# Reordering the opening of a fused AdaLN, spiking mixer and attention kernel on one core: first group, thresholds, a keep-warm run, and the norm of k

## The chip, the cores and the metric

The kernel runs on one core of one Trainium2 chip. A core has TensorE (PE in the profile, its weight loads PEld), VectorE (DVE), ScalarE (ACT), GpSimd (POOL) and SyncE (SP, which here only issues DMAs). The engines run their own instruction streams in program order and meet at semaphores. The metric is the device time of one execution in microseconds; lower is better.

## The reference, cut to what matters

```python
h = layernorm(x) * (1 + ca) + sa                      # x: 2 x 1024 tokens, 128 channels
r = sigmoid(h @ W_r.T + b_r); ek = exp(h @ W_k.T + b_k); v = h @ W_v.T + b_v
# scan over time, td = exp(b_td), g = exp(global_decay)
sa = ek*v + td*sa;  sb = ek + td*sb
inp = r * (g*ek*v + sa) / (g*ek + sb + 1e-6)
reset = mem - .05 > 0;  mem = .3*mem + inp - reset*.05;  spk = mem - .05 > 0
x = x + ga * spk
z = layernorm(x) * (1 + cb) + sb_
for layer in range(2):                                # local attention, 8 heads of 64, window 64
    q, k, v = split(shift_token(z) @ wqkv)
    q, k = l2norm(q) * qs, l2norm(k) * ks;  q, k = rotary_xpos(q, k)
    z = z + softmax(mask(8 * q @ k.T)) @ v @ wo
    z = z + gated_gelu_mlp(layernorm(shift_token(z)))
x = x + gb * z
# then a linear recurrent unit and a mixture of experts (8 experts, top 2), each with its own AdaLN
```

All arithmetic is float32. The change lies in the first block, up to the start of the attention, and in one wait of the attention.

## The kernel before

The 2048 tokens are cut into 4 groups of 512 columns (`g`) for the mixer and the MLPs, and into 16 tiles of 128 tokens (`n`) for the attention of each layer. Activations are stored with channels on the partitions. Every order of work is written out by hand, engine by engine; there is no scheduler.

**The mixer.** For each group, DVE computes the layer norm's statistics (`ln_stats`), POOL the reciprocal root (`ln_rstd`: a power on 128x4, L652, then a product, L653), ACT the normalization of four 128x128 blocks (`ln_norm`, L387), PE turns it back to channels (`ln_t2`), ACT applies the modulation (`mixer_out`, L393), PE makes the products with W_k and W_v (L1431, L1434), ACT the exponential and two scaled copies (L422, L425, L427), and DVE the two scans, the numerator and a reciprocal (from L943 to L957). The modulation vector itself comes from a small product (`modulation`, L1417) and eight small DVE instructions, which end in `mod_fin`. POOL also makes five scalars (`sc_ready`) ahead of its first `ln_rstd`. ACT runs groups 0 and 1 of `mixer_norm` and a table load ahead of `mixer_out(0)`.

**The membrane.** DVE runs four passes of 64 small instructions over 16 interleaved steps (L971, L975) and counts whether the last pass changed anything (L1012, L1013). A one-column product on PE (L1481) sums the count, DVE reads it into a register and branches to a fallback if it isn't zero. A threshold (`threshold`, 128x512) turns the steps into spikes times `ga`; DVE makes groups 0 and 1 (L1017) and POOL 2 and 3 (L777); DVE adds groups 0 and 1 to x (L1050), POOL 2 and 3 (`add_spikes`, L784). PE turns x for the next layer norm (`stack_t1`), the norm's way back is `ln_t2(ln_no(1, g))`, and `stack_out` (L393) writes z. `keep_clock` and `warm` are products without use that keep PE at work in gaps (L1470, L1410).

**The attention.** Per tile PE projects q, k and v (L1459, L1514), DVE multiplies by the rotary tables (L1079, L1082), POOL adds the two halves (`rope_sum`, L801, for k and q), ACT squares q and k, DVE sums the squares (L1093) and clamps them (`clamped`, L1100, then semaphore `ssq_max`), POOL raises them to -1/2 (`norms`, L809), DVE scales q (`q_normed`, L1108) and POOL scales k (`k_normed`, L817). PE turns q and k (`turn_qk`), makes the scores, DVE the maxima (`negmax`, L1114), ACT the exponentials (L515), PE turns them and multiplies with v (`weigh_v`, L1584). POOL's order for a tile is `norms`, a wait for `q_ready` (DVE's scaled q), `k_normed`, two `rope_sum` of the next tile. The first tiles run with a lead of three (`LEAD`): `n == 1 - LEAD` and `n == 2 - LEAD` are the two turns of the loop ahead of tile 0's `weigh_v`.

Of the kernel before, what the change touches and what calls it, by code (L numbers as in the profile page):

```python
# [12 lines left out]
ALU = mybir.AluOpType  # L13
# [8 lines left out]
NG = NTOK // GW  # L22
# [53 lines left out]
def program(nc, a, out):  # L76
    with ExitStack() as ctx:
# [6 lines left out]
        def sem(name):  # L84
# [97 lines left out]

        names = """ld_x0 ld_x1 ld_x2 ld_x3 ld_wm0 ld_wm1 ld_ew ld_c ld_wr ld_wa ld_wq ld_wl ld_lru ld_moe ld_out st_out
            init table edges mod_raw cnt_ready cnt_sum renewed spk hsA_dma1 hsA_dma2 hsA_dma3 silu_c mod_mm mod_fin sc_ready
# [187 lines left out]
        def _(act):  # L372
            act.dma_start(ident[:, :], a["ident"]).then_inc(s["ld_c"], 16)
            act.dma_start(vec[:, :], a["vec"]).then_inc(s["ld_c"], 16)
            own = Steps(act, s["act_own"])

            act.wait_ge(s["ld_c"], 32)
            act.activation(silc[:, :], vec[:, V_C:V_C + 4], ACT.Silu).then_inc(s["silu_c"], 1)
# [28 lines left out]
            def mixer_out(g):  # L407
# [3 lines left out]
                ln_out(ln_no(0, g), hsA[:, gsl(g)], mod[:, 0, CA, b:b + 1], mod[:, 0, SA, b:b + 1])  # L411

            mixer_norm(0)
            mixer_x(0)
            mixer_norm(1)
            act.wait_ge(s["init"], 2)
            load_table(ACT.Exp)
            mixer_out(0)
            for g in range(NG):

                act.wait_ge(s["kv_mm"], 2 * g + 1)
                own.one(act.activation(ek[:, gsl(g)], psS[:, g % 2, :], ACT.Exp, bias=vec[:, V_BK:V_BK + 1]))  # L422
                if g == 0:
                    act.wait_ge(s["sc_ready"], 1)
                act.activation(ek[:, gsl(g)], ek[:, gsl(g)], ACT.Identity, bias=0.0, scale=sc[:, 1:2]).then_inc(s["ek_ready"], 1)  # L425
                act.wait_ge(s["ek_ready"], g + 1)
                act.activation(gek[:, gsl(g)], ek[:, gsl(g)], ACT.Identity, bias=sc[:, 3:4], scale=sc[:, 2:3]).then_inc(s["gek_ready"], 1)  # L427
                if g + 1 < NG:
                    mixer_x(g + 1)
                    mixer_out(g + 1)  # L430
                if g + 2 < NG:
                    mixer_norm(g + 2)
# [204 lines left out]
        def _(pool):  # L637
# [33 lines left out]

            pool.wait_ge(s["ld_c"], 32)
            own.one(pool.memset(fr[:, 0:1], float(np.e)))
# [4 lines left out]
            pool.tensor_scalar(sc[:, 3:4], sc[:, 1:2], 1e-6, 0.0, ALU.mult, ALU.add).then_inc(s["sc_ready"], 1)  # L678
            ln_rstd(ln_no(0, 0))
            ln_rstd(ln_no(0, 1))  # L680
            for dst, src in ((4, V_NU), (5, V_TH), (6, V_GAM)):
# [90 lines left out]
            for k, edge in enumerate((hsA[64:128, T:T + 1], hsA[64:128, 0:1], hsM[64:128, T:T + 1], hsM[64:128, 0:1])):  # L772
                pool.memset(edge, 0.0).then_inc(s["edges"], 1)
                pool.wait_ge(s["edges"], k + 1)
            pool.wait_ge(s["cnt_ready"], 1)
            for g in (2, 3):
                pool.tensor_scalar(by_chunk(ekv, g), of_group(ph, g, 1), -1.0, mod[:, 0, GA, bof(g):bof(g) + 1],  # L777
                                   ALU.is_lt, ALU.mult).then_inc(s["spk"], 1)

            def add_spikes(g):  # L780

                pool.wait_ge(s["spk"], g - 1)
                pool.wait_ge(s["x_mixed"], g)
                pool.tensor_tensor(x_cm[:, gsl(g)], x_cm[:, gsl(g)], ekv[:, gsl(g)], ALU.add).then_inc(s["x_mixed"], 1)  # L784

# [34 lines left out]
            def attention(l, i):  # L820

                n = l * NT + i
                if has(i + 2):
                    norms(n + 2)
                    pool.wait_ge(s["q_ready"], n + 3)
                    k_normed(n + 2)
                if has(i + 3):
                    rope_sum(n + 3, 1)
                    rope_sum(n + 3, 0)
# [60 lines left out]
        def _(dve):  # L890
# [23 lines left out]
            mixer_stats(1)  # L914
            dve.wait_ge(s["ld_c"], 32)
            def modulation(k, bank):
# [105 lines left out]
            own.one(dve.tensor_copy(cnti[0:1, 0:1], psT1[0:1, 0:1]))  # L1022
            threshold(own, 1)
            changed = dve.value_load(cnti[0:1, 0:1], min_val=0, max_val=P * B * NCH)
            with dve.If(changed != 0):

                dve.wait_ge(s["cnt_ready"], 1)
                dve.wait_ge(s["spk"], 2)
                own.sync()
                again = [Steps(dve, s["fallback"]), Steps(dve, s["fallback_b"])]  # L1030
                for b in range(B):
                    again[b].did(dve.memset(vst[:, b, :], 0.0))
                changed = checked_pass(again)
                with dve.If(changed != 0):
                    with dve.Fori(0, NCH) as k:
                        for st in again:
                            st.enter(k, 2 * SEQ)
                        membrane_pass(again)
                    for st in again:
                        st.leave(NCH)  # L1040
                        st.sync()
                renewed = Steps(dve, s["renewed"])
                for g in range(NG):
                    threshold(renewed, g)
                renewed.sync()
# [8 lines left out]
            add_spikes(1)  # L1054
            for g in range(NG):
                ln(ln_no(1, g))

# [78 lines left out]
            dve.wait_ge(s["ln_out"], ln_no(1, 0) + 1)  # L1136
            shifted(hsA, z, 0, "hsA_ready")
            dve.wait_ge(s["rope_ready"], 4)
            qk_first(0)
# [234 lines left out]
        def _(pe):  # L1374
# [17 lines left out]

            pe.wait_ge(s["ld_c"], 32)

# [12 lines left out]
            def warm(times):  # L1407

                for _ in range(times):
                    mm(psO[:, 0, 0:P], ident[:, :], ident[:, :], start=True, stop=True)  # L1410

            mixer_turn(0)
            pe.wait_ge(s["silu_c"], 1)
# [6 lines left out]

            warm(6)
            modulation(0, psQK[:, 0, :])
            warm(4)

            ln_t2(ln_no(0, 0))
            pe.wait_ge(s["ld_wr"], 16)
            for g in range(NG):
# [61 lines left out]
            stack_t1(1)  # L1489
            keep_clock(2, psT1[:, :])  # L1490
            stack_t1(2)
            keep_clock(8, psT1[:, :])
            stack_t1(3)
            ln_t2(ln_no(1, 0))
            keep_clock(4, psT1[:, :])
# [19 lines left out]

            def turn_qk(l, i, between=None):

# [9 lines left out]
                four(psT0, lambda k: qkn[:, k * P:(k + 1) * P]).then_inc(s["qT_fill"], 1)  # L1527
                if between is not None:
                    between()
                pe.wait_ge(s["k_ready"], n + 1)  # L1530
# [75 lines left out]
            def attention(l, i):  # L1606
# [20 lines left out]
                if n == 1 - LEAD:  # L1627
                    proj_v(0, 0)
                    proj_part(0, 2, 1)
                    turn_qk(0, 0, lambda: proj_part(0, 2, 0))  # L1630
                    ln_t2(ln_no(1, NG - 1))
                elif early:
                    turn_qk(l, 0)
                    proj_v(l, 0)
                elif has(i + 2):
                    proj_v(l, i + 2)
                    turn_qk(l, i + 2)
                if i == NT - 1:
# [289 lines left out]
```

## Time and profile before

| | us |
|---|---|
| time before, median of 3 runs | 572.86 |
| lowest and highest of the three | 572.21, 574.23 |
| the profiled execution: its time | 573.93 |
| the profiled execution: its span | 572.1 |
| membrane passes, first instruction to the count | 49.8 to 85.8 |
| attention of layer 1, first to last `weigh_v` | 123.5 to 234.8 |
| attention of layer 2, first to last `weigh_v` | 295.4 to 408.2 |

Times in rows count from the start of the span. What lies around the span (573.93 less 572.1, 1.8 us) stays out of reach of the change. A row of the timeline is: start, length, engine, line, operation, output and inputs with their shapes, count of instructions merged into the row, and in brackets the idle time of the engine ahead of it and what ended it. For merged rows the length is that of the whole row.

### The profile page before, as it was taken

How to read it: one execution, taken by the hardware profiler on the slowest of the kernel's cores; microseconds unless marked ns; L12 is line 12 of the kernel's file. 1: busy time of each engine (PE TensorE's matmuls, PEld its weight loads, DVE VectorE, ACT ScalarE, POOL GpSimd, SP SyncE). 2: the span in 40 equal slices, each digit the busy share in tenths (PEclk: the TensorE clock that was granted, in tenths of full speed). 3: DMA queues.
4: the chain of work that ended last, by engine and by line, in shares of the span. 5: the costliest groups of instructions: out<-in, count | busy, mean ns of one | idle time of the engine just before them, and what ended most of it. 6: DMA issues, size and time to landing. Idle time of an engine off the chain costs nothing. (4 is left out here: it accounts for less than half of the span.)

```text
span 572.1 us, 11749 instructions
## 1 busy us (share of the span) xinstructions
PE 491.3 (86%) x4026; PEld 309.5 (54%) x4026; DVE 437.4 (76%) x1179; ACT 347.6 (61%) x1001; POOL 316.3 (55%) x257
## 2 busy tenths in 40 slices
PE   4741037889999999999989999999999998999995
PEld 4311013457777776543457777776544445667774
DVE  6699997879999995546899999995445687457775
ACT  4771002679999997543479999997646525533331
POOL 6551008788888888576888888884010275110000
PEclk9795558989999999999999999999999999999999
DMA  8400002221111112000031111111000000000000
GB/s 290 153 1 1 1 1 75 47 46 40 38 40 39 38 40 69 16 1 1 1 111 41 38 39 34 35 38 38 1 2 0 0 1 1 1 0 19 21 18 19
DMA packets 14832, 19.93 MB, mean 35 GB/s; under 512 B 2314, under 2 KB 8948, under 8 KB 14644
## 3 DMA queue, kind: packets, MB, share of 16 engines
q1 hardware_dynamic: 14484, 19.08, 12.2%
q8 instruction: 33, 0.54, 0.4%
q14 instruction: 27, 0.22, 0.1%
q10 hardware_dynamic: 288, 0.08, 0.1%
HBM read 8.94 MB, written 1.05 MB: 17 GB/s over the span
## 5 line engine op out<-in xcount | busy, mean ns | idle before, releaser
L515 ACT ACTIVATE prob<-psS,nmx 128x128 f32<-128x128 f32 x256 | 89.9, 377 | 19.8 <-DVE nmx L1114 19.8
L809 POOL TENSOR_TENSOR rn<-ssq,half 128x16 f32<-128x16 f32 x32 | 93.2, 2911 | 4.0 <-DVE ssq L1100 1.1
L801 POOL TENSOR_TENSOR ra<-ra,rb 128x512 f32<-128x512 f32 x64 | 80.1, 1273 | 2.7 <-DVE rb L1082 2.7
L652 POOL TENSOR_TENSOR rst<-mv,half 128x4 f32<-128x4 f32 x24 | 25.3, 1053 | 73.9 <-DVE mv L903 62.6
L1459 PE MATMUL psQK<-wqkv,hsA 128*128 128x512 f32 x128 | 62.2, 605 | 1.6 <-DVE hsA L1063 1.2
L515 ACT ACTIVATION_READ_ACCUMULATOR prob<-psS,nmx 128x1 f32 x256 | 55.4, 216 | 0.0
L1079 DVE TENSOR_TENSOR ra<-psQK,rope 128x512 f32<-128x512 f32 x64 | 43.9, 686 | 6.6 <-PE psQK L1459 5.9
L817 POOL TENSOR_TENSOR qkn<-ra,rn 128x512 f32<-128x512 f32 x32 | 33.3, 1042 | 26.4 <-DVE qkn L1108 26.4
L1114 DVE TENSOR_REDUCE nmx<-psS 128x4 f32<-128x512 f32 x64 | 41.1, 683 | 3.5 <-PE psS L1564 3.4
L1082 DVE TENSOR_TENSOR rb<-psQK,rope 128x512 f32<-128x512 f32 x64 | 43.6, 681 | 0.0
L633 ACT ACTIVATE gel<-psQK 128x512 f32<-128x512 f32 x32 | 19.1, 596 | 39.8 <-PE psQK L1772 39.8
L1378 PEld LDWEIGHTS psT<-ident,qkn 128*128 128x128 f32 x256 | 30.1, 142 | 24.1 <-issue 14.8
L1093 DVE TENSOR_REDUCE ssq<-sq 128x8 f32<-128x512 f32 x64 | 41.1, 676 | 1.1 <-ACT sq L455 0.9
L387 ACT ACTIVATE lnx<-psS,nmr,rst 128x128 f32<-128x128 f32 x20 | 7.5, 456 | 55.2 <-POOL nmr L653 55.2
L489 ACT ACTIVATE pT<-psT 128x512 f32<-128x512 f32 x64 | 36.4, 654 | 4.9 <-PE psT L1378 4.9
L1378 PE MATMUL psT<-ident,qkn 128*128 128x128 f32 x256 | 34.6, 276 | 5.0 <-DVE qkn L1108 3.8
L1584 PE MATMUL psO<-vAB,pT 128*64 128x64 f32 x1024 | 36.9, 225 | 1.6 <-ACT pT L489 1.6
L1378 PEld LDWEIGHTS psT<-ident,prob 128*128 128x128 f32 x256 | 29.8, 140 | 15.0 <-issue 14.4
L1470 PE MATMUL psO<-masks,identb 128*128 128x512 bf16 x22 | 7.8, 527 | 33.5 <-DVE vAB L975 33.5
L1584 PEld LDWEIGHTS psO<-vAB,pT 128*64 128x64 f32 x1024 | 32.4, 138 | 7.7 <-ACT pT L489 5.6
L1514 PE MATMUL psO<-wqkv,hsA 128*128 128x512 f32 x64 | 35.8, 641 | 0.0
L1108 DVE TENSOR_TENSOR qkn<-ra,rn 128x512 f32<-128x512 f32 x32 | 22.1, 691 | 16.9 <-POOL rn L809 16.8
(238 smaller groups left out, 1203.7 us busy)
## 6 DMA issues: line engine op xcount, KB each, us to landing
vAB<-vAB SPq DMA_DIRECT2D x62, 128.0 KB, 2.2
wqkv<-in_wqkv SPq DMA_DIRECT2D x2, 768.0 KB, 8.2
big<-in_x SPq DMA_DIRECT2D x4, 256.0 KB, 4.6
ropeb<-in_rope SPq DMA_DIRECT2D x1, 1024.0 KB, 6.4
big<-in_ew SPq DMA_DIRECT2D x2, 512.0 KB, 4.2
out<-big SPq DMA_DIRECT2D x4, 256.0 KB, 2.3
wmod<-in_wmod SPq DMA_DIRECT2D x2, 384.0 KB, 5.9
w<-in_w SPq DMA_DIRECT2D x2, 341.0 KB
```

The source lines that it names most:

```text
L489: act.activation(pT[:, 4 * hb:4 * hb + 4, :], four((psT0, psT1)[hb]), ACT.Copy).then_inc(s["pT_evac"], 1)
L515: act.activation(prob[:, k, :], psS[:, hb, c * P:(c + 1) * P], ACT.Exp, bias=nmx[:, k:k + 1], accum_out=sums[:, n % 2, k:k + 1]).then_inc( ...
L801: pool.tensor_tensor(o, o, rb[:, r], ALU.add).then_inc(s["sum_" + name], 1)
L809: pool.tensor_tensor(rn[:, :], ssq[:, :], half[:, :], ALU.pow).then_inc(s["rn_ready"], 1)
L1079: dve.tensor_tensor(heads(o), heads(psQK[:, part, :]), rope[:, at8, 2 * part, :].unsqueeze(1).to_broadcast([P, H, DH]), ALU.mult).then_inc ...
L1082: dve.tensor_tensor(rb[:, r].rearrange("p (h a d) -> p h a d", h=H, a=2), psQK[:, part, :].rearrange("p (h a d) -> p h a d", h=H, a=2)[:, ...
L1093: dve.tensor_reduce(ssq[:, 8 * part:8 * part + 8], heads(sq[:, part * INNER:(part + 1) * INNER]), AX.X, ALU.add).then_inc(s["ssq_" + name], 1)
L1114: dve.tensor_reduce(nmx[:, 4 * hb:4 * hb + 4], psS[:, hb, :].rearrange("p (h k) -> p h k", h=4), AX.X, ALU.max, negate=True).then_inc(s["n ...
L1378: i = pe.transpose(dst[:, k * P:(k + 1) * P], src(k), ident[:, :])
L1459: mm(psQK[:, part, :], hsA[:, tile(i)], wqkv[:, part * INNER:(part + 1) * INNER], start=True, stop=True).then_inc(s[name + "_mm"], 1)
L1514: mm(psO[:, 1, :], hsA[:, tile(i)], wqkv[:, 2 * INNER:3 * INNER], start=True, stop=True).then_inc(s["v_fill"], 1)
L1584: j = mm(psO[64 * w:64 * w + 64, 0, h * DH:(h + 1) * DH], pT[:, slot(h), 64 * w:64 * w + 64], (vA, vB)[w][:, u, h * DH:(h + 1) * DH], star ...
```

## The change

It has these parts:

- **First group.** ident has a semaphore of its own (`ld_id`), so PE waits for it alone; three `warm` products go ahead of the first turn, three ahead of the modulation, two behind `ln_t2(0)` in place of four ahead of it. POOL runs `ln_rstd` 0 and 1 ahead of its scalars. ACT loads the table first and runs `mixer_norm(1)` behind group 0's exponential and copies instead of ahead of `mixer_out(0)`.
- **Thresholds.** All four on DVE: 0, 1 and 2 around the reading of the count, 3 behind the statistics of group 0; POOL keeps the adds of groups 2 and 3. The statistics of group 3 go behind the shift of group 0.
- **First way back.** `ln_t2(ln_no(1, 0))` goes ahead of `stack_t1(3)`; `keep_clock` runs of 2 and 8 are joined to one of 10 ahead of it.
- **Into the attention.** `keep_clock(3)` ahead of the first `turn_qk`, q's projection of tile 2 behind it; `ln_t2(ln_no(1, 3))` moves one turn later, behind the first scores; `keep_clock(8)` ahead of the second `turn_qk`.
- **Norm of k.** POOL's wait for `q_ready` ahead of `k_normed` is gone, in both layers.

```diff
@@ scalar
-            mixer_norm(0)
-            mixer_x(0)
-            mixer_norm(1)
-            act.wait_ge(s["init"], 2)
-            load_table(ACT.Exp)
+            act.wait_ge(s["init"], 1)
+            load_table(ACT.Exp)
+            mixer_norm(0)
+            mixer_x(0)
             mixer_out(0)
...
+                if g == 0:
+                    mixer_norm(1)
                 if g + 1 < NG:
@@ gpsimd
-            pool.wait_ge(s["ld_c"], 32)
+            ln_rstd(ln_no(0, 0))
+            ln_rstd(ln_no(0, 1))
+            pool.wait_ge(s["ld_c"], 16)
...
-            ln_rstd(ln_no(0, 0))
-            ln_rstd(ln_no(0, 1))
...
-            pool.wait_ge(s["cnt_ready"], 1)
-            for g in (2, 3):
-                pool.tensor_scalar(by_chunk(ekv, g), of_group(ph, g, 1), -1.0, mod[:, 0, GA, bof(g):bof(g) + 1],
-                                   ALU.is_lt, ALU.mult).then_inc(s["spk"], 1)
-
             def add_spikes(g):
 
-                pool.wait_ge(s["spk"], g - 1)
                 pool.wait_ge(s["x_mixed"], g)
+                if g == 3:
+                    pool.wait_ge(s["spk"], 1)
...
                     norms(n + 2)
-                    pool.wait_ge(s["q_ready"], n + 3)
                     k_normed(n + 2)
@@ vector
             threshold(own, 1)
+            threshold(own, 2)
             changed = dve.value_load(cnti[0:1, 0:1], min_val=0, max_val=P * B * NCH)
...
-            for g in range(NG):
-                ln(ln_no(1, g))
+            ln(ln_no(1, 0))
+            threshold(Steps(dve, s["spk"]), 3)
+            ln(ln_no(1, 1))
+            ln(ln_no(1, 2))
...
             shifted(hsA, z, 0, "hsA_ready")
+            ln(ln_no(1, 3))
@@ tensor
-            pe.wait_ge(s["ld_c"], 32)
+            pe.wait_ge(s["ld_id"], 16)
...
+            warm(3)
             mixer_turn(0)
...
-            warm(6)
+            warm(3)
             modulation(0, psQK[:, 0, :])
-            warm(4)
-
             ln_t2(ln_no(0, 0))
+            warm(2)
...
-            keep_clock(2, psT1[:, :])
             stack_t1(2)
-            keep_clock(8, psT1[:, :])
+            keep_clock(10, psT1[:, :])
+            ln_t2(ln_no(1, 0))
             stack_t1(3)
-            ln_t2(ln_no(1, 0))
             keep_clock(4, psT1[:, :])
...
                 if n == 1 - LEAD:
                     proj_v(0, 0)
                     proj_part(0, 2, 1)
-                    turn_qk(0, 0, lambda: proj_part(0, 2, 0))
-                    ln_t2(ln_no(1, NG - 1))
+                    keep_clock(3, psT1[:, :])
+                    turn_qk(0, 0)
+                    proj_part(0, 2, 0)
...
                 elif has(i + 2):
+                    if n == 2 - LEAD:
+                        ln_t2(ln_no(1, NG - 1))
                     proj_v(l, i + 2)
+                    if n == 2 - LEAD:
+                        pe.wait_ge(s["kT_evac"], 1)
+                        keep_clock(8, psT1[:, :])
                     turn_qk(l, i + 2)
```

## Rows read from the trace of the kernel before

**Rows 1.** Waits of POOL, whole span: us in total, times, longest

```profile
POOL qkn L817 <- DVE qkn L1108: 26.4, 32, 1.3
```

**Rows 2.** Timeline, one tile of layer 1 in the attention

```profile
164.05 2.91 POOL L809 TENSOR_TENSOR rn<-ssq,half 128x16 f32<-128x16 f32 x1
...
166.99 0.69 DVE L1108 TENSOR_TENSOR qkn<-ra,rn 128x512 f32<-128x512 f32 x1 [0.28 <-POOL rn L809]
...
167.06 1.15 PE L1584 MATMUL psO<-vAB,pT 128*64 128x64 f32 x32
...
167.76 1.04 POOL L817 TENSOR_TENSOR qkn<-ra,rn 128x512 f32<-128x512 f32 x1 [0.81 <-DVE qkn L1108]
...
168.76 2.50 POOL L801 TENSOR_TENSOR ra<-ra,rb 128x512 f32<-128x512 f32 x2
...
171.01 0.29 DVE L1100 TENSOR_SCALAR ssq<-ssq 128x16 f32<-128x16 f32 x1
...
171.38 2.91 POOL L809 TENSOR_TENSOR rn<-ssq,half 128x16 f32<-128x16 f32 x1
...
174.32 1.15 PE L1584 MATMUL psO<-vAB,pT 128*64 128x64 f32 x32
```

**Rows 3.** Timeline, two tiles of layer 2, PE's products with v

```profile
303.64 1.15 PE L1584 MATMUL psO<-vAB,pT 128*64 128x64 f32 x32
...
310.96 1.15 PE L1584 MATMUL psO<-vAB,pT 128*64 128x64 f32 x32
```

**Rows 4.** Timeline, the mixer's first group and the start of its second

```profile
5.71 0.16 DVE L903 TENSOR_SCALAR mv<-mv 128x4 f32<-128x4 f32 x1
...
7.55 1.04 POOL L652 TENSOR_TENSOR rst<-mv,half 128x4 f32<-128x4 f32 x1
...
8.90 1.65 ACT L387 ACTIVATE lnx<-big,nmr,rst 128x128 f32<-128x128 f32 x4 [3.76 <-POOL nmr L653]
...
13.99 0.76 ACT L393 ACTIVATE hsA<-psT,mod 128x512 f32<-128x512 f32 x1
...
14.89 1.94 PE L1431 MATMUL psS<-hsA,wrkv 128*128 128x512 f32 x2 [3.63 <-ACT hsA L393]
...
17.59 0.72 ACT L425 ACTIVATE big<-big,sc 128x512 f32<-128x512 f32 x1
...
18.58 0.76 DVE L943 SCALAR_TENSOR_TENSOR psO<-psO,vec,big 128x512 f32<-128x512 f32 x1 [4.72 <-PE psO L1434]
...
20.36 1.12 PE L1431 MATMUL psS<-hsA,wrkv 128*128 128x512 f32 x2 [0.94 <-ACT hsA L393]
...
25.67 0.67 DVE L943 SCALAR_TENSOR_TENSOR psO<-psO,vec,big 128x512 f32<-128x512 f32 x1
```

**Rows 5.** Timeline, from the thresholds to the first z

```profile
85.99 5.80 POOL L777 TENSOR_SCALAR big<-vAB,mod 128x512 f32<-128x512 f32 x2 [40.02 <-DVE cnt L1013]
...
86.51 1.47 DVE L1017 TENSOR_SCALAR big<-vAB,mod 128x512 f32<-128x512 f32 x1
...
91.04 0.89 DVE L897 BATCH_NORM_STATS2 st<-psS 128x6 f32<-128x128 f32 x4
...
92.97 1.03 POOL L652 TENSOR_TENSOR rst<-mv,half 128x4 f32<-128x4 f32 x1
...
93.59 3.54 PE L1470 MATMUL psT<-masks,identb 128*128 128x512 bf16 x8
...
98.05 0.78 ACT L393 ACTIVATE z<-psO,mod 128x512 f32<-128x512 f32 x1 [2.23 <-PE psO L1378]
```

**Rows 6.** Timeline, first norm of the attention and first product with v

```profile
105.55 2.91 POOL L809 TENSOR_TENSOR rn<-ssq,half 128x16 f32<-128x16 f32 x1 [0.36 <-DVE ssq L1100]
...
123.55 1.15 PE L1584 MATMUL psO<-vAB,pT 128*64 128x64 f32 x32
```

**Rows 7.** Timeline, late in the kernel: two instructions that read SBUF twice, together

```profile
466.21 0.69 DVE L1272 TENSOR_TENSOR big<-z,big 128x512 f32<-128x512 f32 x1
466.25 1.78 POOL L867 TENSOR_TENSOR big<-z,tsin 128x512 f32<-128x512 f32 x1 [2.02 <-DVE z L1267]
```

More of the change, by code:

```diff
@@ L181, in program @@
         psT1 = ps("psT1", [P, GW])
-        names = """ld_x0 ld_x1 ld_x2 ld_x3 ld_wm0 ld_wm1 ld_ew ld_c ld_wr ld_wa ld_wq ld_wl ld_lru ld_moe ld_out st_out
+        names = """ld_id ld_x0 ld_x1 ld_x2 ld_x3 ld_wm0 ld_wm1 ld_ew ld_c ld_wr ld_wa ld_wq ld_wl ld_lru ld_moe ld_out st_out
             init table edges mod_raw cnt_ready cnt_sum renewed spk hsA_dma1 hsA_dma2 hsA_dma3 silu_c mod_mm mod_fin sc_ready
@@ L372, in _ @@
         def _(act):
-            act.dma_start(ident[:, :], a["ident"]).then_inc(s["ld_c"], 16)
+            act.dma_start(ident[:, :], a["ident"]).then_inc(s["ld_id"], 16)
             act.dma_start(vec[:, :], a["vec"]).then_inc(s["ld_c"], 16)
             own = Steps(act, s["act_own"])
-            act.wait_ge(s["ld_c"], 32)
+            act.wait_ge(s["ld_c"], 16)
             act.activation(silc[:, :], vec[:, V_C:V_C + 4], ACT.Silu).then_inc(s["silu_c"], 1)
@@ L914, in _ @@
             mixer_stats(1)
-            dve.wait_ge(s["ld_c"], 32)
+            dve.wait_ge(s["ld_c"], 16)
             def modulation(k, bank):
@@ L1027, in _ @@
                 dve.wait_ge(s["cnt_ready"], 1)
-                dve.wait_ge(s["spk"], 2)
                 own.sync()
@@ L1042, in _ @@
                 renewed = Steps(dve, s["renewed"])
-                for g in range(NG):
+                for g in range(NG - 1):
                     threshold(renewed, g)
@@ L1054, in _ @@
             add_spikes(1)
-            for g in range(NG):
-                ln(ln_no(1, g))
+            ln(ln_no(1, 0))
+            threshold(Steps(dve, s["spk"]), 3)
+            ln(ln_no(1, 1))
+            ln(ln_no(1, 2))
             def shifted(dst, src, g, name):
@@ L1514, in proj_v, with turn_qk @@
                 mm(psO[:, 1, :], hsA[:, tile(i)], wqkv[:, 2 * INNER:3 * INNER], start=True, stop=True).then_inc(s["v_fill"], 1)
-            def turn_qk(l, i, between=None):
+            def turn_qk(l, i):
                 n = l * NT + i
@@ L1527, in turn_qk @@
                 four(psT0, lambda k: qkn[:, k * P:(k + 1) * P]).then_inc(s["qT_fill"], 1)
-                if between is not None:
-                    between()
                 pe.wait_ge(s["k_ready"], n + 1)
```

## The prediction, made before the result was seen

> **What bounds the kernel now.** I read the timeline stage by stage, since the change touches an opening that runs in chains (0 to 124 us) and one wait of the attention. The chain that ended last reaches back only to the expert stage, which stays as it is, so an early gain moves the end only if nothing between absorbs it. In the membrane passes DVE alone works; they shift as a block.
>
> In the attention three loops nearly coincide. PE's own tile is 174.32 - 167.06 = 7.26 us, with no wait shown [rows 2]. POOL's tile is 171.38 - 164.05 = 7.33: the power 2.91, then 0.81 of waiting until DVE has scaled q, k's norm 1.04, two sums 2.50, and the clamp, which got in only when the second sum had ended at 171.26 [rows 2]. That wait comes to 26.4 us over 32 tiles [rows 1], but PE could give at most 7.33 - 7.26 a tile back. In layer 2 PE's tile is 7.32, paced by that loop [rows 3].
>
> **The first group.** GpSimd starts the power of group 0 at 7.55, though the statistics were there at 5.87; its scalars stood ahead [rows 4]. With the order turned it starts at 5.95, the normalization at 7.3 instead of 8.90, and ends at 8.95 [rows 4]. The table load now lies ahead of that, in ACT's idle time (3.76 us there). The way back on PE is over at about 9.7; `mod_fin` is there at about 10.1 by my estimate: PE starts when ident has landed and not vec, and the modulation, with one turn and six `warm` products ahead of it as now, moves up by that, some 0.8. So `mixer_out(0)` starts at 10.1 instead of 13.99: 3.9 less. Here nothing of group 1 and no table load stands between. PE's first pair of products took 1.94 for k after 3.63 us of idleness, and 1.12 in the second group [rows 4]; with `warm` and no such gap the engine stays at the upper clock level, some 0.9 less (bounds 0 and 1.6). From 10.1: 0.76, product 1.1, exponential and copy 1.4 give 13.4 for DVE's first instruction, against 18.58. What is late next is the second group: DVE needs 25.67 - 18.58 = 7.09 for a group and would be ready at 20.5, but ACT has then run group 1's normalization (1.65), its modulation, group 2's normalization (1.65) and the exponential, and I add it up to 20.95. From there on DVE is the bound as before, and I take **4.7 us** (25.67 - 20.95; bounds 3.5 and 5.2). The scalars, now behind the powers, end at about 11.5, with ACT asking at 12.7. The copy of x needs neither.
>
> **Thresholds and the first way back.** Two thresholds held GpSimd to 91.79 [rows 5]; then came its first add, and the power of the attention's first norm at 92.97, while its statistics were over at 91.04, where the next group's begin [rows 5]. On DVE the third threshold costs 0.7, but the second took 1.47 while GpSimd worked on the same tile, and should take 0.7 alone, so DVE's adds start where they did. If reading the register and branching was hidden under those 1.47 and shows again behind the third, up to 0.7 is lost. DVE's two adds, behind 86.51 + 1.47 = 87.98 at some 0.65 each, end at 89.3 [rows 5]; GpSimd then adds group 2 until 90.7 (1.25, the length of its sums [rows 2]) and is free: the power starts at 91.1, 1.85 earlier, and the normalization is over at 93.95. The eight useless products took 3.54 [rows 5], at the lower clock level after a gap; without it ten take 2.3 and end at 93.5, in front of `ln_t2(ln_no(1, 0))`, which no longer waits for `stack_t1(3)`. z starts at 94.7 instead of 98.05 [rows 5], 3.35 less. DVE has threshold 3 (0.7 to 1.5) and two statistics to finish by 95.5 and just does; group 3's statistics (1.6) then fill the gap in which it waited for PE, at a cost of 0.1. I take **3.3 us** up to the first power on `rn`, 102.25 instead of 105.55 [rows 6]; bounds 1.6 (branch and a late threshold) and 4.0.
>
> **The wait ahead of k's norm.** It goes in 32 places, but not its whole 0.81 us comes back. Both instructions read SBUF twice (the sums or ra, and rn). [Rows 7] show such a pair: DVE started 0.04 us ahead and took its usual 0.69, GpSimd took 1.78 and ended 1.13 behind DVE's end; a GpSimd instruction of that shape takes 1.25 [rows 2]. So it was blocked, and only its 0.1 to 0.2 of start-up ran under the other.
> That is what the Trainium skill, SBUF — State Buffer, Who interferes with whom, states: a DVE instruction with two SBUF inputs and a GpSimd instruction that reads SBUF exclude each other, and whichever starts first holds the shared ports throughout. By this rule each tile gets 0.1 to 0.2 back; by rows 2 read without it, 0.8. The trace agrees with the rule.
> DVE starts 0.03 us behind the power's end (164.05 + 2.91 = 166.96, then 166.99) [rows 2]; GpSimd starts 0.08 behind what releases it (the clamp ends at 171.01 + 0.29 = 171.30, the power starts at 171.38) [rows 2]. So DVE goes first where it is waiting, and k's norm ends 0.2 earlier. POOL's loop becomes about 7.2 (7.33 less 0.15), DVE's through the clamp is the same, and PE paces all at 7.26. That is worth 0.07 for the last five tiles of layer 1 and 14 of layer 2: 0.35 and 1.0.
>
> In the lead-in of layer 1 each of two powers comes 0.1 to 0.2 earlier, `keep_clock(8)` saves a stretch at the lower level on PE, but DVE's clamp, maxima and ACT's exponentials, which now stand behind z of group 3, gain only 3.2. The first loops pass through these, so of the possible 5 us at 123.55 [rows 6] I keep 3.65 a tile later: **0.35** more (bounds -1.0 and +2.5, the latter if the 0.8 came back each time). In layer 2's lead-in DVE is behind with the MLP when the power ends; there GpSimd goes first, and q is blocked for up to 1.04 [rows 2]: **-0.6** (bounds -1.6 and +0.6).
>
> **Sum.** 4.7 + 3.3 + 0.35 + 0.35 + 1.0 - 0.6 = 9.1 us. The profiled execution, 573.93 (span 572.1 and 1.8 around it), would be 564.8. It lies 1.1 above the median of the runs, 572.86, so the prediction is 572.86 - 9.1 = 563.8.
>
> **Rivals.**
> *The port turned against q.* Should GpSimd win at the power's end, where 0.05 us decides, q's scaling starts 1.1 later in each tile, and DVE's loop, 7.2 with that scaling in it, becomes 8.3. Over 30 tiles that is 30 x 1.0 = 30 us against today's 7.33: 572.9 - 9 + 30, about 592. For it speaks that both wait for the same instruction; against it the 0.03 against 0.08, and that DVE works on tables and then waits 0.28 [rows 2]. It decides from the point at which DVE's start falls behind by 0.05 in more than ten tiles. Chance 0.07. The same rule in the Trainium skill (SBUF — State Buffer, Who interferes with whom) gives this too, since there the order decides.
> *No exclusion.* The pair runs together and k's norm ends 0.8 earlier: lead-ins give 2.5 and 0.6 instead of 0.35 and -0.6, so 572.9 - 12.5 = 560.4. Against it are rows 7. Chance 0.10.
> *The second gain is absorbed.* The branch shows behind the third threshold (0.7), threshold 3 stands in front of the statistics with GpSimd's powers beside it (1 us), and the lead-in falls to the lower clock (1 to 1.5): 3 to 3.5 less, 567.2. For it: DVE is on the path throughout that stretch. Chance 0.20.
> *The change doesn't do what it says.* Group 1's later normalization makes DVE wait for group 1 as long as it gained on group 0 and the thresholds only change engine: 572 to 573. ACT's sum for group 1 is within 0.5 us of DVE's, so it would take a further 4 us that no row shows. Chance 0.03.
>
> **How the numbers follow.** My forecast has 0.60, with 561.8 to 566 as its own range. To this the range adds the absorbed case and the case without exclusion, nearly whole: 560.5 to 568, holding about 0.85 (0.60 + 0.20 + part of 0.10). The port turned against q and no effect stay outside. A measurement of this kernel tells about 0.3% (1.7 us) from no change. Faster: 0.60 + 0.10 + 0.20 + what of the rest is a mild form = 0.91; same 0.03; slower 0.06.
>
> **What would show it.** In the profile after: `mixer_out(0)` at about 10.1, DVE's group 1 at about 21, the first membrane instruction near 45.1 instead of 49.8; the power of the first attention norm 1.8 earlier against the count and z 3.3; no useless product above 0.3 us before z; k's norm with a length near 1.7 where it starts within 0.1 us of q's, and ending 0.2 earlier against the power; PE's tile 7.26 in both layers. The prediction is wrong if q's norm is seen starting behind k's (tile above 7.4), if DVE's adds start more than 0.5 later against the count, or if DVE waits for ACT in group 1.

## The result, and the profile after

| | before | after |
|---|---|---|
| time, median of 4 runs | 572.57 | 566.70 |
| lowest and highest | 572.21, 574.23 | 566.26, 567.15 |
| the profiled execution: time and span | 573.93, 572.1 | 566.38, 564.4 |
| start of the membrane's count (its last instruction) | 85.5 | 82.9 |
| first power on `rn` | 105.55 | 99.94 |
| layer 1, first to last `weigh_v` | 123.5 to 234.8 | 115.9 to 227.8 |
| layer 2, first to last `weigh_v` | 295.4 to 408.2 | 288.8 to 400.4 |

The ratio of after to before is 0.9895, with an interval of 0.988 to 0.991: faster by 1.0%, 5.9 us between the medians (the median of before is now over one run more than at the time of the forecast). The forecast was 563.8 with a range of 560.5 to 568.0. The time lies in the range, but 0.7 above the likeliest case's own range (561.8 to 566), near the 567.2 of the absorbed case. The prediction also named a wait of DVE for ACT in group 1 as a sign of being wrong; the profile shows one of 0.18 us, at 22.93 below.

In the timeline after, the first group (answers to [rows 4]); the clock record of this trace begins at 15.56 with the upper level:

```profile
6.05 1.02 POOL L653 TENSOR_TENSOR rst<-mv,half 128x4 f32<-128x4 f32 x1 [4.30 <-DVE mv L899]
...
7.39 1.65 ACT L387 ACTIVATE lnx<-big,nmr,rst 128x128 f32<-128x128 f32 x4 [0.90 <-POOL nmr L654]
...
10.67 0.15 DVE L923 COPY zero<-mod 128x1 f32<-128x1 f32 x1
...
10.86 0.78 ACT L393 ACTIVATE hsA<-psT,mod 128x512 f32<-128x512 f32 x1 [1.34 <-DVE zero L923]
...
11.78 2.04 PE L1430 MATMUL psS<-hsA,wrkv 128*128 128x512 f32 x2 [0.35 <-ACT hsA L393]
...
13.62 1.91 PE L1433 MATMUL psO<-hsA,wrkv 128*128 128x512 f32 x2
...
15.57 0.76 DVE L939 SCALAR_TENSOR_TENSOR psO<-psO,vec,big 128x512 f32<-128x512 f32 x1 [1.82 <-PE psO L1433]
...
22.93 0.76 DVE L939 SCALAR_TENSOR_TENSOR psO<-psO,vec,big 128x512 f32<-128x512 f32 x1 [0.18 <-ACT big L424]
```

The normalization starts 1.5 earlier, about as forecast. Two things eat into it: `mixer_out(0)` waits 1.34 for the modulation vector, and both products take nearly twice what the product with W_k takes at the upper level of TensorE's clock (2.04 and 1.91 against 1.12 in [rows 4]). DVE waits for the second of them.

The timeline after, from the thresholds to the first power on `rn` (answers to [rows 5, 6]):

```profile
83.87 1.30 DVE L1013 TENSOR_SCALAR big<-vAB,mod 128x512 f32<-128x512 f32 x2
...
85.47 1.29 DVE L1046 TENSOR_TENSOR x_cm<-x_cm,big 128x512 f32<-128x512 f32 x2 [0.30 <-DVE big L1013]
...
86.91 1.26 POOL L781 TENSOR_TENSOR x_cm<-x_cm,big 128x512 f32<-128x512 f32 x1 [43.14 <-DVE x_cm L1046]
...
88.40 0.69 DVE L1013 TENSOR_SCALAR big<-vAB,mod 128x512 f32<-128x512 f32 x1
88.57 1.41 POOL L653 TENSOR_TENSOR rst<-mv,half 128x4 f32<-128x4 f32 x1 [0.40 <-DVE mv L899]
...
88.72 2.32 PE L1469 MATMUL psT<-masks,identb 128*128 128x512 bf16 x10
...
90.21 1.26 POOL L781 TENSOR_TENSOR x_cm<-x_cm,big 128x512 f32<-128x512 f32 x1
...
90.34 1.16 DVE L898 TENSOR_SCALAR nmean<-mv 128x4 f32<-128x4 f32 x1
...
92.55 0.78 ACT L393 ACTIVATE z<-psO,mod 128x512 f32<-128x512 f32 x1 [0.75 <-PE psO L1377]
...
99.94 2.91 POOL L806 TENSOR_TENSOR rn<-ssq,half 128x16 f32<-128x16 f32 x1 [0.28 <-DVE ssq L1098]
```

Against the count, z is 98.05 - 92.55 - 2.6 = 2.9 earlier. The second and third threshold take 1.30 together, reading the register and branching show 0.30 behind them, and the ten useless products take 2.32 at the upper level (the granted clock is 1.00 from 83.8 to 99.9).

The timeline after, one tile of layer 1 (answers to [rows 2]):

```profile
128.42 2.91 POOL L806 TENSOR_TENSOR rn<-ssq,half 128x16 f32<-128x16 f32 x1 [0.21 <-DVE ssq L1098]
...
131.36 0.69 DVE L1106 TENSOR_TENSOR qkn<-ra,rn 128x512 f32<-128x512 f32 x1 [0.31 <-POOL rn L806]
...
131.40 1.15 PE L1580 MATMUL psO<-vAB,pT 128*64 128x64 f32 x32
131.40 1.55 POOL L814 TENSOR_TENSOR qkn<-ra,rn 128x512 f32<-128x512 f32 x1
...
132.91 2.50 POOL L798 TENSOR_TENSOR ra<-ra,rb 128x512 f32<-128x512 f32 x2
...
135.38 0.17 DVE L1098 TENSOR_SCALAR ssq<-ssq 128x16 f32<-128x16 f32 x1
...
135.63 2.90 POOL L806 TENSOR_TENSOR rn<-ssq,half 128x16 f32<-128x16 f32 x1 [0.21 <-DVE ssq L1098]
...
138.66 1.15 PE L1580 MATMUL psO<-vAB,pT 128*64 128x64 f32 x32
```

The wait of 26.4 us [rows 1] is gone, and k's norm now takes 1.55 and not 1.04: it starts 0.04 behind q's and mostly stands still until that is over. From the power's start to its end it is 4.53 against 4.75 in [rows 2], 0.22 earlier. POOL's tile is 7.21 and PE's 7.26.

q's norm keeps its 0.68 to 0.69 in 31 of the 32 tiles. In the second tile of layer 2 GpSimd was first by 0.02, and q's norm was the one that was blocked:

```profile
282.12 1.04 POOL L814 TENSOR_TENSOR qkn<-ra,rn 128x512 f32<-128x512 f32 x1
282.14 1.57 DVE L1106 TENSOR_TENSOR qkn<-ra,rn 128x512 f32<-128x512 f32 x1
```

### The profile page after: what moved, and what is told of

Same layout as the page of the kernel before. It is cut to its first block and busy times, and to the rows that moved or that the text cites. A ratio compares the mean times of both kernels' runs of the same rounds, so it can differ in the third digit from the quotient of the medians.

```text
span 564.4 us, 11730 instructions
## 1 busy us (share of the span) xinstructions
PE 491.8 (87%) x4033; PEld 310.3 (55%) x4033; DVE 436.7 (77%) x1181; ACT 348.3 (62%) x1001; POOL 328.7 (58%) x255
## 5 line engine op out<-in xcount | busy, mean ns | idle before, releaser
L814 POOL TENSOR_TENSOR qkn<-ra,rn 128x512 f32<-128x512 f32 x32 | 49.5, 1548 | 2.5
L1377 PEld LDWEIGHTS psT<-ident,prob 128*128 128x128 f32 x256 | 29.8, 140 | 14.8 <-issue 14.3
L1215 DVE SCALAR_TENSOR_TENSOR hg<-psO,vec,gel 128x512 f32<-128x512 f32 (+1 forms) x24 | 17.2, 745 | 20.9 <-ACT gel L569 20.9
```

Source lines behind the costliest of these rows:

```text
L814: pool.tensor_tensor(heads(qkn[:, INNER:]), heads(ra_k[n % 2]), rn[:, 8:16].unsqueeze(2).to_broadcast([P, H, DH]), ALU.mult).then_inc(s["k ...
L1377: i = pe.transpose(dst[:, k * P:(k + 1) * P], src(k), ident[:, :])
```

## The experiments

Each was compared with the kernel before on its own chip; the ratios are to that. Marks in the traces (count, first power on `rn`, first and last `weigh_v`) are read as in the table above.

**The parts alone, on the kernel before.** First the wait ahead of k's norm:

```diff
                     norms(n + 2)
-                    pool.wait_ge(s["q_ready"], n + 3)
                     k_normed(n + 2)
```

> The kernel before with only the wait for q_ready ahead of k's norm taken out, both layers. Theory 1 (the two norms exclude each other at SBUF, q's goes first): k's norm grows from 1.04 to about 1.55 us and ends only 0.3 earlier against the power; PE's tile in layer 2 goes from 7.33 to 7.26, 1.0 to 1.2 us over the layer, and the time falls by 1 to 2 us. Theory 2 (they run side by side): k's norm keeps 1.04, the power's period in the lead-ins falls to 6.5, the time falls by 3.5 us or more.

Measured: 572.99 against 573.01, ratio 0.9996 (0.9985 to 1.0008). k's norm is 1.55 long here too. Layer 2 takes 111.6 instead of 112.8, as expected, but the stretch between the layers is 0.7 longer and layer 1 is unchanged; no gain can be told, where 1 to 2 us were expected. GpSimd was first in three of the 32 tiles, two of them in the first four of layer 1, and q's norm took 1.39 to 1.57 there. In the profiled execution the mixer's first DVE instruction stood at 17.7, not at 18.58.

The first group's edits alone (the diff's lines on `ld_id`, the order of POOL's scalars, table and `mixer_norm(1)` on ACT, `warm`):

> The kernel before with only the mixer's first group reordered (ident's own semaphore, warm 3+3+2, powers ahead of the scalars, table first, group 1's normalization behind group 0's copies). Theory 1: DVE's first mixer instruction comes 3 us earlier (15.6 instead of 18.6), its chain runs without waits from there and everything behind is shifted: 2.7 us less. Theory 2 (given back later): the count comes 2.7 earlier, but PE's clock level falls in other places of the lead-in and at most 1 us is left at the end.

Measured: 570.96, ratio 0.9958 (0.9945 to 0.9972), 2.4 us, near the 2.7 of theory 1. DVE started at 15.5 and the count came at 82.9, both as in the changed kernel.

The thresholds, `keep_clock(10)`, `ln_t2(ln_no(1, 0))` ahead of `stack_t1(3)` and the later statistics of group 3 alone:

> The kernel before with only the thresholds on DVE, group 3's statistics behind the shift, ten keep_clock products and the first way back ahead of the fourth turn. Theory 1: from the count to the first power on rn 3.0 us less (20.0 before), as in the changed kernel, and 2.5 to 3 us at the end. Theory 2 (absorbed in the lead-in, where other things bound): 3.0 to the first power, under 1.5 at the end.

Measured: 571.24, ratio 0.9961 (0.9949 to 0.9973), 2.2 us, a little under theory 1. The first power on `rn` came 17.1 behind the count, as in the changed kernel, instead of 20.0.

The way into the attention alone (`keep_clock(3)` and `(8)`, `ln_t2(ln_no(1, 3))` a turn later):

> The kernel before with only the edits on PE in the lead-in of layer 1 (keep_clock 3 and 8, q's projection of tile 2 behind the first turn, group 3's way back one turn later). Theory 1: the second keep-warm run saves the stretch at the lower clock ahead of the first product with v, 1 us, and z of group 3, now behind the first scores on ACT, gives most of it back: 0 to 1 us less. Theory 2: z of group 3 on ACT costs more than the clock gives: up to 1 us more.

Measured: 573.33, ratio 0.9999 (0.9989 to 1.001). The first `weigh_v` came 1.6 earlier against the count (36.4 instead of 38.0) and layer 1 took 1.6 more (112.9 instead of 111.3): the head start was handed back at POOL's 7.33 a tile.

The four ratios leave 0.42 + 0.39 + 0.04 + 0.01 = 0.86%, 4.9 us, against 6.0 by the ratio together. The missing 1.1 us is within the intervals, but the next run shows an interaction of two parts of about that size.

**The changed kernel with the wait put back.**

```diff
                     norms(n + 2)
+                    pool.wait_ge(s["q_ready"], n + 3)
                     k_normed(n + 2)
```

> The changed kernel with the wait for q_ready ahead of k's norm put back. Theory 1 (the lead-in's 1.5 us stays only if the loop of GpSimd is a little faster than PE's): layer 1 from first to last product with v grows from 111.9 to about 113, layer 2 from 111.6 to 112.8, the seam between the layers gets 0.5 shorter; 568.3 to 568.8. Theory 2 (the wait has nothing to do with it, as alone it gave nothing measurable): 566.5 to 567.

Measured: 568.41, ratio 0.9927 (0.9911 to 0.9944). Taking the wait away is worth 0.32%, 1.8 us, here. Layer 1 takes 112.8 with it and 111.9 without, layer 2 112.8 and 111.6. Alone, taking the wait away was worth 0.04% and changed nothing in layer 1. Behind the edits of the way into the attention, with which GpSimd's loop of 7.33 sets the pace from the first tiles on, it gives 0.9 there. That is the interaction of the two parts; by the ratios it is 0.28%, 1.6 us, with an uncertainty nearly as large.

**q's norm made to start second.** The changed kernel, and the same edit in the kernel of the run above as a control:

```diff
                 dve.wait_ge(s["rn_ready"], n + 1)
+                own.one(dve.memset(zero[:, 0:1], 0.0))
                 dve.wait_ge(s["sum_q"], n + 1)
```

> The changed kernel with one small VectorE instruction (a memset of one column, and the wait for it) between the power's end and q's norm, so that k's norm on GpSimd starts first. Theory 1 (exclusive ports, the first to start holds them): q's norm starts or ends about 1.0 later against the power, VectorE's loop has 8.2 to 8.3 us a tile, PE's tile follows, 25 to 30 us more: 592 to 597. Theory 2 (order does not matter, or the two share the ports in parts): only the small instruction is paid, 0.15 us a tile at most, 567 to 569.

> Control for q_second: the same small VectorE instruction with the wait for q_ready put back, so that q's norm is later by it but never against k's. Both theories: 0.15 us a tile on the loop of GpSimd, 7.33 to about 7.5: 571 to 573.

Measured: 589.89, ratio 1.0306 (1.0283 to 1.0329), and for the control 572.26, ratio 0.9995 (0.9983 to 1.0007). The timeline of the first, one tile:

```profile
154.53 2.90 POOL L806 TENSOR_TENSOR rn<-ssq,half 128x16 f32<-128x16 f32 x1 [1.23 <-DVE ssq L1098]
...
157.50 0.06 DVE L1103 MEMSET zero<- 128x1 f32 x1 [0.42 <-POOL rn L806]
157.51 1.04 POOL L814 TENSOR_TENSOR qkn<-ra,rn 128x512 f32<-128x512 f32 x1
157.59 1.51 DVE L1107 TENSOR_TENSOR qkn<-ra,rn 128x512 f32<-128x512 f32 x1
...
162.68 2.91 POOL L806 TENSOR_TENSOR rn<-ssq,half 128x16 f32<-128x16 f32 x1 [1.22 <-DVE ssq L1098]
```

Now GpSimd has its usual 1.04 and DVE takes 1.51 for its 0.69. The tile is 8.15 instead of 7.25, and the time lies 2 us below the range of theory 1 (592 to 597). The instruction in front costs 3.9 us where the order is held (572.26 less 568.41); where it turns the order it costs 23.2 (589.89 less 566.70). The order of two starts, 0.08 apart, is worth 19 us here. By this the exclusion of [rows 7] is shown for this pair too, and so is the price of the rival of the port turned against q (592 forecast), which only a few hundredths of a microsecond keep away. The Trainium skill's rule (SBUF — State Buffer, Who interferes with whom) is borne out in both orders.

**Why the first group started at 15.6 and not at 13.4.** The changed kernel with the modulation straight behind the first turn:

```diff
-            warm(3)
             modulation(0, psQK[:, 0, :])
+            warm(6)
             ln_t2(ln_no(0, 0))
             warm(2)
```

> The changed kernel with the modulation's products straight behind the first turn and six warm products behind them, ahead of ln_t2(0), instead of three ahead of the modulation. Theory 1 (the first group is bound by mod_fin and then by PE at the lower clock level): mod_fin comes 0.7 to 1.3 earlier, and six products in a row right ahead of the group's own raise the level before the product with W_k; VectorE's first mixer instruction at 13.5 to 14.5 instead of 15.6, 1 to 2 us less in the end (564.7 to 565.7). Theory 2 (the second group's chain on ScalarE is next): VectorE then waits for the exponential of group 1, and 0.5 at most is left.

Measured: 567.75, ratio 0.9914 (0.9896 to 0.9932): no gain. Its timeline:

```profile
8.17 2.91 PE L1409 MATMUL psO<-ident 128*128 128x128 f32 x12
...
9.36 0.15 DVE L923 COPY zero<-mod 128x1 f32<-128x1 f32 x1
...
10.87 1.06 PE L1377 MATMUL psT<-ident,lnx 128*128 128x128 f32 x4
...
12.04 0.78 ACT L393 ACTIVATE hsA<-psT,mod 128x512 f32<-128x512 f32 x1 [2.55 <-PE psT L1377]
...
12.96 1.10 PE L1430 MATMUL psS<-hsA,wrkv 128*128 128x512 f32 x2 [0.34 <-ACT hsA L393]
...
15.65 0.76 DVE L939 SCALAR_TENSOR_TENSOR psO<-psO,vec,big 128x512 f32<-128x512 f32 x1 [3.21 <-ACT big L424]
```

In this execution the vector is there at 9.51 and the product with W_k is at the upper level, 1.10 long, as theory 1 has it. But the six useless products stood in front of the way back until 10.87. So they were split, which brings the run to the point:

```diff
-            warm(3)
             modulation(0, psQK[:, 0, :])
+            warm(2)
             ln_t2(ln_no(0, 0))
-            warm(2)
+            warm(3)
```

> The changed kernel, with the modulation straight behind the first turn, two useless products behind it (four passes, some 1.0 us, until about 9.1, when the normalization of group 0 is over) and three behind the way back; one useless product less in all than now. With six of them behind the modulation nothing was gained, and I hold that those six, twelve passes of 2.91 us, stood themselves in front of the way back. My theory: mod_fin at about 9.5, way back over at about 10.2, mixer_out(0) at 10.3 instead of 10.86, PE at work without a gap from 5.75 to 11.2, so that the product with W_k takes 1.10 as with six of them (and not 2.04); DVE's first mixer instruction 3.6 behind mixer_out(0), at about 13.9 instead of 15.57, and 565.2 to 565.7 us, 1.2 less than the changed kernel (0.2 to 0.4 of the 1.7 is lost where DVE waits for ACT in the second group). Rival one: the start stays at 15.6, since fewer passes keep the granted clock at the lower level until 15.5: 566.4 to 566.9. Rival two: DVE starts at 13.9 and waits for ACT in group 1 as long as it gained: 566.4 as well, with a wait of over 1 us ahead of group 1.

Measured: 566.23, ratio 0.9893 (0.9876 to 0.9911). Its timeline:

```profile
10.29 0.78 ACT L393 ACTIVATE hsA<-psT,mod 128x512 f32<-128x512 f32 x1 [0.86 <-PE psT L1377]
...
11.26 1.57 PE L1430 MATMUL psS<-hsA,wrkv 128*128 128x512 f32 x2
...
14.43 0.76 DVE L939 SCALAR_TENSOR_TENSOR psO<-psO,vec,big 128x512 f32<-128x512 f32 x1 [1.97 <-ACT big L424]
...
18.80 3.35 DVE L953 RECIPROCAL big<-big 128x512 f32<-128x512 f32 x1 [0.44 <-POOL big L704]
...
22.07 0.67 DVE L939 SCALAR_TENSOR_TENSOR psO<-psO,vec,big 128x512 f32<-128x512 f32 x1
...
22.78 1.99 DVE L945 TENSOR_TENSOR_SCAN big<-sc,big 128x512 f32<-128x512 f32 x1
```

DVE starts 1.14 earlier than in the changed kernel, but the count comes only 0.2 earlier (82.7), and the time is the same. The expected loss to ACT is not there; a third engine, GpSimd, takes the gain. The reciprocal of group 0 waits 0.44 for GpSimd's denominator (L704), and the scan of group 1, which started at 23.72 and took 1.28 in the changed kernel, falls beside GpSimd's rotary tables and takes 1.99. That the split itself brought DVE's earlier start is not shown. Seven profiled executions, each of a different kernel, have the changed kernel's own opening. In four DVE started at 15.4 to 15.6 (the changed kernel, the first group alone, the wait put back, the kernel without the way into the attention), in three at 14.5 (both kernels with the memset, and the next one). The opening of the next kernel:

```profile
9.04 0.66 PE L1377 MATMUL psT<-ident,lnx 128*128 128x128 f32 x4 [0.38 <-ACT lnx L387]
...
9.90 0.78 ACT L393 ACTIVATE hsA<-psT,mod 128x512 f32<-128x512 f32 x1 [0.43 <-DVE zero L923]
...
10.83 1.96 PE L1430 MATMUL psS<-hsA,wrkv 128*128 128x512 f32 x2 [0.68 <-ACT hsA L393]
...
14.52 0.76 DVE L939 SCALAR_TENSOR_TENSOR psO<-psO,vec,big 128x512 f32<-128x512 f32 x1 [1.72 <-PE psO L1433]
```

The way back takes 0.66 here against 1.09 in the changed kernel's trace, and the modulation vector is there at 9.87 and not at 10.82: in this execution TensorE was already at the upper level. Then PE stood idle for 0.68, and the granted clock is 0.50 from 10.9 to 14.3. Its reciprocal of group 0 waited 0.59 for GpSimd and its scan of group 1 took 1.97, so it lost the earlier start in the same two places. The count came at 82.6 in the three early executions and at 82.9 to 83.6 in the four others.

**Threshold 3 one group later.**

```diff
             ln(ln_no(1, 0))
-            threshold(Steps(dve, s["spk"]), 3)
             ln(ln_no(1, 1))
+            threshold(Steps(dve, s["spk"]), 3)
```

> The changed kernel, with threshold 3 behind the statistics of group 1 instead of group 0. My theory: in the changed kernel it ran beside the power of group 0's norm (1.41 long and not 1.03) and pushed GpSimd's add of group 3 onto the negated mean of group 1, which took 1.16. With it one group later the power takes 1.03, the normalization of group 0 and z come 0.4 earlier (z 2.5 less than before by the count, now 2.87 after 5.5 against 2.63), and the end 0.4: 566.2 us against 566.7, which five rounds can hardly tell; the lengths of the power and of the negated mean decide. Rival one: the threshold, now beside GpSimd's power again or beside the add, only moves the block to another instruction: z the same, 566.7. Rival two: group 3's add comes later and with it the fourth way back: 567.2.

Measured: 566.44, ratio 0.9895 (0.9877 to 0.9913). Its timeline:

```profile
88.31 1.02 POOL L653 TENSOR_TENSOR rst<-mv,half 128x4 f32<-128x4 f32 x1 [0.40 <-DVE mv L899]
...
89.48 0.17 DVE L898 TENSOR_SCALAR nmean<-mv 128x4 f32<-128x4 f32 x1
...
89.63 0.69 DVE L1013 TENSOR_SCALAR big<-vAB,mod 128x512 f32<-128x512 f32 x1
...
91.90 0.78 ACT L393 ACTIVATE z<-psO,mod 128x512 f32<-128x512 f32 x1 [0.75 <-PE psO L1377]
```

The power is back to 1.02 and the negated mean to 0.17. From DVE's two adds (85.22 here) to z it is 6.68 instead of 92.55 - 85.47 = 7.08, the 0.4 of the theory. The time agrees with the theory but can't be told from no change.

**The changed kernel without the edits of the way into the attention.**

```diff
-                    keep_clock(3, psT1[:, :])
-                    turn_qk(0, 0)
-                    proj_part(0, 2, 0)
+                    turn_qk(0, 0, lambda: proj_part(0, 2, 0))
+                    ln_t2(ln_no(1, NG - 1))
...
-                    if n == 2 - LEAD:
-                        ln_t2(ln_no(1, NG - 1))
                     proj_v(l, i + 2)
-                    if n == 2 - LEAD:
-                        pe.wait_ge(s["kT_evac"], 1)
-                        keep_clock(8, psT1[:, :])
```

> The changed kernel without the edits of the way into the attention (the old order of the two turns ahead of tile 0's product with v, no keep_clock(3) and keep_clock(8)); first group, thresholds and k's norm are as changed. Alone on the kernel before, those edits gained 1.5 us up to the first product with v and gave it back in layer 1 (112.8 instead of 111.3), where I hold GpSimd's loop with k's wait to set 7.3 a tile. My theory: with the wait gone layer 1 takes the gain on: without the edits the first product with v comes 1.5 later against the count and layer 1 takes 111.3 instead of 111.9, so 0.9 us more than the changed kernel, 567.6. Rival: the edits are worth nothing here as well, 566.7 (first product with v 1.5 later, layer 1 at 110.4).

Measured: 567.49, ratio 0.9908 (0.989 to 0.9926). The time is the one expected, the way to it is not. The first `weigh_v` came 33.5 behind the count and not 34.5 (33.0 in the changed kernel), layer 1 took 111.4, and the stretch between the layers was 62.5 instead of 61.0, with the granted clock at the lower level from 284.7 to 288.1, which the changed kernel's trace does not have there. GpSimd was first in three tiles of this execution (110.64, 282.85 and 290.34), with q's norm 1.38 to 1.57 long, and in one of the changed kernel's, so part of the longer stretch between the layers is q's norm blocked. What these edits are worth beside the others stays open: 0.8 us by the medians, with intervals that overlap.

**GpSimd relieved in the mixer.** The two better variants together, and GpSimd's work that is not wanted yet moved out of the way:

```diff
@@ gpsimd, in place of ahead of the powers of groups 2 and 3
                 if g == 0:
-                    rope_tables(0)
+                    rope_tables(0, range(3))
                 if g == 1:
                     quotient(0)
+                    rope_tables(0, range(3, 4))
+                    for dst, src in ((4, V_NU), (5, V_TH), (6, V_GAM)):
+                        own.did(pool.tensor_tensor(sc[:, dst:dst + 1], fr[:, 0:1], vec[:, src:src + 1], ALU.pow))
+                    own.sync()
+                    own.one(pool.tensor_scalar(fr[:, 2:3], sc[:, 4:5], -1.0, 0.0, ALU.mult, ALU.add))
+                    own.one(pool.tensor_tensor(sc[:, 7:8], fr[:, 0:1], fr[:, 2:3], ALU.pow))
```

> The changed kernel with the split useless products (modulation, two, way back, three) and threshold 3 behind the statistics of group 1, and besides with GpSimd relieved in the mixer: the five scalars of the recurrent unit (2.4 us) go out of the way of the denominator of group 0 to behind the quotient of group 0, and of the four rotary tables the last goes there too, so that none lies beside the scan of group 1. With the split alone DVE began 1.14 earlier and the count came only 0.2 earlier: the reciprocal of group 0 waited 0.44 for GpSimd's denominator and the first scan of group 1 took 1.99 and not 1.24. My theory: GpSimd was what came late next, so now the reciprocal of group 0 has no wait and starts at 18.3, the scan of group 1 takes 1.24, DVE's groups start at 14.4, 21.6, 28.7 and 35.8 and the count is at 81.3 to 81.6 instead of 82.9; with 0.35 more from the threshold the first power on rn comes at 98.1 instead of 99.9 and the time is 564.9, 1.8 less than the changed kernel. Rival: ACT and PE come late next, DVE waits for the exponential of group 1 or 2 by as much, the count is at 82.6 and the time 566.1.

Measured: 565.54, ratio 0.9869 (0.9853 to 0.9886), from four runs: 565.33, 565.47, 565.61 and, the profiled one, 567.13. It is the lowest of all the kernels here, 7.5 us under before by the ratio; its interval still touches that of the changed kernel. The trace is of the slowest of the four and shows both theories at work:

```profile
18.94 3.34 DVE L954 RECIPROCAL big<-big 128x512 f32<-128x512 f32 x1
...
23.24 0.76 DVE L940 SCALAR_TENSOR_TENSOR psO<-psO,vec,big 128x512 f32<-128x512 f32 x1 [0.95 <-PE psO L1434]
...
24.03 1.28 DVE L946 TENSOR_TENSOR_SCAN big<-sc,big 128x512 f32<-128x512 f32 x1
...
36.27 0.63 ACT L437 ACTIVATE big<-big 128x512 f32<-128x512 f32 x1
...
37.04 3.48 POOL L694 TENSOR_TENSOR z<-big 128x512 f32<-128x512 f32 x2 [2.00 <-ACT big L437]
...
42.99 3.35 DVE L954 RECIPROCAL big<-big 128x512 f32<-128x512 f32 x1 [1.59 <-POOL big L699]
```

The reciprocal of group 0 has no wait and the scan of group 1 takes 1.28: GpSimd was what came late. But DVE started at 15.11 in this execution, where the same order of work on PE gave 14.43 in the run with the split products, and the granted clock is 0.50 from 16.9 to 23.7; PE's products for group 1 took 2.08 and 1.92 in it, and DVE waited 0.95 for them; the sigmoids followed late, GpSimd's two products behind them took 3.48 and held up the denominator of group 3 for 1.59. The count came at 84.0 in this execution. Whether the other three, 1.5 to 1.8 faster, had the count at 81.5 no trace shows.

## Why the prediction was right, and what it got wrong

By the profiled executions the gain is 573.93 - 566.38 = 7.55 us, by the medians 5.9; 9.1 was forecast. That the time still fell inside the range is in part luck: the first group was forecast 2 us too high, and the attention about 1 us too low.

- **The first group: mis-sized, 4.7 forecast, 2.7 measured** (25.67 - 22.93; 2.6 at the count). GpSimd, the table load and group 1's normalization went as forecast. Of the 2.17 by which DVE's start missed 13.4, the vector accounts for 0.76 (`mixer_out(0)` at 10.86, not 10.1): the modulation's products took 2.56, where they took 1.40 in the kernel before. The product with W_k took 2.04 where I had put 1.1. My sentence "with `warm` and no such gap the engine stays at the upper clock level" failed: PE was at work nearly without a gap from 3.49 to 11.43, and it still ran the pair at 2.04. Another 0.3 is the product with W_v, at the lower level as well, on which DVE waited and not on the exponential. In the three executions with the same opening that started DVE at 14.5, the vector came in time (`mixer_out(0)` at 9.90 to 9.95), but the product with W_k took 1.89 to 1.96 all the same. So about half of the 2.17 belongs to the execution, and the rest to a clock level that the forecast had too high. The first membrane instruction came at 47.2 instead of 49.8; 45.1 was forecast.
- **"From there on DVE is the bound as before" fails for any earlier start**, and that weighs more than the late start. With a start at 14.4 the count moved by 0.2. GpSimd's denominator and its tables beside the scan take the rest. I take from this that even a start at 13.4 would not have given 20.95 for group 1; no run shows such a start. I had added up ACT's work for group 1, and not GpSimd's for group 0.
- **Thresholds and first way back: right, 3.3 forecast, 3.0 measured** (105.55 - 99.94 - 2.64). The adds start where they did, the branch shows with 0.30 (up to 0.7 allowed for), the ten products took 2.32 (2.3 forecast), z came 2.9 earlier against the count (3.35). The 0.4 missing is threshold 3 beside the power: with it moved, z came 3.3 earlier.
- **Layer 1: too low, and by another way.** I kept 0.35 for the lead-in and 0.35 for the end: 0.7 from the first power on `rn` to the last `weigh_v`. It was 7.0 - 5.6 = 1.4: the first `weigh_v` came 7.7 earlier, and layer 1 gave back 0.6. PE paces it at 7.26 as forecast.
- **Layer 2: +1.0 and -0.6 forecast, +0.8 measured** (408.2 - 400.4 less 7.0). Within the layer it is 1.2, between the layers -0.4, and nothing after it is lost.
- **k's norm: right.** Blocked, 1.55 long, ending 0.22 earlier, q first by 0.04, POOL's tile 7.21. The case without exclusion is out, since k's norm would have kept its 1.04. The port turned against q in one tile of 32, in the lead-in of layer 2, where the forecast had it; in the other 31 it did not, and the memset turned it in every tile. The forecast of 592 for that case is mis-added: 572.9 - 9 + 30 is 593.9.
- **The profile's execution as the base: wrong by about 1.** I took 9.1 from the median, as if the 1.1 by which that execution lay above the median were spread evenly. Much of it lay in the opening which the change replaces: DVE's first mixer instruction stood at 18.58 there, and at 17.7, 17.5 and 18.0 in the profiles of the three kernels above that keep this opening (the wait, the thresholds and the way into the attention alone). From 17.7 there is 0.9 less to gain.

So the shortfall of 3.2 us against the medians is 2.1 (first group) + 0.3 (thresholds) - 1.0 (more gained in the attention) + 1.8, the rest, which is nearly all the base: the profiled execution of before lay 1.4 above its median over four runs, that of after 0.3 below. The rival of the second gain absorbed came nearest in time, but it was the first gain that was absorbed: the second came nearly whole.

## What to carry to other kernels

When an early stage is sped up on one engine, add up all the engines that feed the next instruction of the bound, the one with spare time too; and look at what their work will then lie beside, since two instructions that exclude each other only cost where they meet. Removing a wait between two such instructions gives back a start-up time and not the wait, and leaves the order to a race of a few hundredths of a microsecond which here costs ten times the gain (19 us against 1.8). And do not subtract a sum made in one execution from a median before asking in which stage that execution was slow.

## What the runs showed of the hardware that was not expected

- Two instructions that both read SBUF twice: GpSimd second gives 1.55 for its 1.04, DVE second 1.51 for its 0.69; each starts 0.04 to 0.08 behind the other and ends 0.90 and 0.55 behind it, so only 0.14 of its own length runs beside the first.
- A DVE instruction on 4 columns took 1.16 instead of 0.17 (90.34, `nmean`) beside a GpSimd add of 1.26: it ended with the add, however little it had to do itself.
- TensorE ran nearly without a gap from 3.49 to 11.43 in the changed kernel, and its products took the length of the lower level until 15.5. The same opening, instruction for instruction, had its way back, at about 9.0, at the length of the upper level in three other executions (0.66 against 1.09), with the lower level back from 10.9 after an idle stretch of about 0.7. What the engine did up to 7 us is the same in both, so the order of work alone did not decide the level here.
- That opening started DVE at 15.4 to 15.6 in four executions and at 14.5 in three, of kernels that differ only later. The granted clock in the mixer also fell at other places in nearly every trace (at 16.9, 19.0, 29.3 and 36.0, for example).
